# A four-layer float32 transformer pass: the second attention's keys, ones, residuals, token sums and score banks rearranged

## What is computed

```python
x = x + L0_attention(layernorm(x))          # one head of width 256
x = x + L0_experts(layernorm(x))            # 12 experts, top 3; each sequence's output is scaled by 0.2
                                            # where sigmoid(relu(mean_tokens(out) @ Wp1 + bp1) @ Wp2 + bp2) > 0.7
x = x + L1_attention(layernorm(x), kv_k, kv_v)   # 16 heads of width 16 over 4096 given keys
x = x + L1_experts(layernorm(x))            # 8 experts, top 2, and a shared one

# L1_attention
Q = (query @ Wq.T) in heads;  scores = Q K^T / 4;  out = softmax(scores) V;  return out @ Wo.T
```

## Time and profile before

| | |
|---|---|
| median of 3 runs | 2233.84 us (2232.94 to 2234.01) |
| profiled execution | 2250.17 us, its span 2248.4 us |
| busy in the span | PE 2017.5 us, DVE 1573.8, ACT 1361.0, POOL 260.1 |
| mean granted TensorE clock | 0.930 of 2.4 GHz |
| costliest groups | DVE maxima 1241.2 us (1024 of 1224 ns), ACT exponentials 1108.4 (2048 of 595 ns), PE values 650.8, scores 523.6, maxima products 438.5 |

### The profile page before, as it was taken

The page is one execution under the profiler, slowest core; times in us unless marked ns, Lnnn a source line. Parts: engine busy times, 40 slices in busy tenths (PEclk is TensorE's granted clock), DMA queues, the critical chain, the costliest instruction groups (busy, mean ns, idle before and its releaser), DMA issues. The chain is left out here.

```text
span 2248.4 us, 40077 instructions
## 1 busy us (share of the span) xinstructions
PE 2017.5 (90%) x15956; PEld 1006.2 (45%) x15956; DVE 1573.8 (70%) x1951; ACT 1361.0 (61%) x2700; POOL 260.1 (12%) x274
## 2 busy tenths in 40 slices
PE   6793999992478999999999999999999999999984
PEld 3552889991222333333333333333333333446663
DVE  2337212215587999998999999999999999315344
ACT  1220444440114888887888888888888888673221
POOL 0000434431020000000000000000000000002462
PEclk9795999995665999999999999999999999999997
DMA  4201677765815000006100006000002000001124
GB/s 139 84 5 66 211 227 255 254 193 138 107 45 69 6 9 13 13 1 69 13 1 14 13 1 69 13 2 13 13 18 64 2 2 1 17 16 34 59 83 154
DMA packets 150034, 140.93 MB, mean 63 GB/s; under 512 B 75506, under 2 KB 122590, under 8 KB 149086
## 3 DMA queue, kind: packets, MB, share of 16 engines
q1 hardware_dynamic: 140446, 112.72, 21.3%
q0 software_dynamic: 9408, 25.70, 3.5%
HBM read 106.40 MB, written 31.72 MB: 61 GB/s over the span
## 5 line engine op out<-in xcount | busy, mean ns | idle before, releaser
L1003 DVE TENSOR_REDUCE maxp<-banks 128x2 f32<-128x1024 f32 x1024 | 1241.2, 1224 | 73.8 <-PE banks L997 72.8
L1435 ACT ACTIVATE pring<-banks 128x512 f32<-128x512 f32 x2048 | 1108.4, 595 | 231.1 <-PE banks L1316 117.6
L1330 PE MATMUL banks<-pring,vcur 128*17 128x256 f32 x8192 | 650.8, 390 | 7.9 <-ACT osb L1429 3.6
L1316 PE MATMUL banks<-qst,kst 50*128 50x512 f32 x2048 | 523.6, 502 | 6.9 <-PEq L1074 5.4
L997 PE MATMUL banks<-kst,qst 48*128 48x512 f32 x2048 | 438.5, 426 | 29.6 <-DVE maxp L1003 26.4
L1316 PEld LDWEIGHTS banks<-qst,kst 50*128 50x128 f32 x2048 | 199.3, 185 | 448.7 <-ACT pring L1435 416.4
L1330 PEld LDWEIGHTS banks<-pring,vcur 128*17 128x17 f32 x8192 | 137.1, 96 | 369.2 <-issue 202.6
L997 PEld LDWEIGHTS banks<-kst,qst 48*128 48x128 f32 x2048 | 202.1, 194 | 76.7 <-DVE maxp L1003 68.8
L766 ACT ACTIVATE hT<-banks,b 128x128 f32<-128x128 f32 x295 | 108.1, 367 | 187.8 <-PE banks L703 172.2
L904 DVE TENSOR_SCALAR yo<-banks,wblock 128x256 f32<-128x256 f32 x59 | 28.5, 484 | 223.8 <-PE banks L712 223.8
L1301 POOL TENSOR_TENSOR acc<-xn,orec 128x256 f32<-128x256 f32 x15 | 9.3, 620 | 1254.9 <-DVE orec L1480 1254.9
(11 more groups left out here) (304 smaller groups left out, 1306.0 us busy)
## 6 DMA issues: line engine op xcount, KB each, us to landing
w1r<-in_L_ffn_w SPq DMA_DIRECT2D x59, 640.0 KB
kst<-key_parts SPq DMA_DIRECT2D x24, 512.0 KB, 17.6
key_parts<-ksp SPq DMA_DIRECT2D x32, 256.0 KB
w2all<-in_L_ffn_w SPq DMA_DIRECT2D x12, 640.0 KB, 7.7
w2all<-expert_rows SPq DMA_DIRECT2D x12, 512.0 KB, 8.7
qst<-query_parts SPq DMA_DIRECT2D x96, 64.0 KB, 2.3
normed_rows<-xn SPq DMA_DIRECT2D x8, 512.0 KB, 2.9
kf<-in_kT SPq DMA_DIRECT2D x16, 256.0 KB
```

Of the source, the lines that this page charges most:

```text
L1003: return nc.vector.tensor_reduce(maxp[:, B % 2, :, hp, qt, kb], ps[:, base:base + 2, :], X, ALU.max)
L1316: nc.tensor.matmul(ps[:, n % 3, :], kst[g % 2][rows, j // 2, kt * P:(kt + 1) * P], qst[i][rows, j // 2, :], start=True, stop=True).then_in ...
L1330: mm = nc.tensor.matmul(ps[32 * j:32 * j + VC, 7, cols], vcur[g % 2][:, kt, j, :], pring[:, (G % 2) * HG + j, cols], start=(kt == 0 and ha ...
L1435: nc.scalar.activation(pring[:, n % (2 * HG), :], ps[:, n % 3, :], ACT.Exp, scale=float(DH) ** -0.5).then_inc(exp_done, 1)
```

## The change

- The token sums: VectorE's four reductions into `xn` go; TensorE sums `acc` over tokens in the experts' block, one group of eight products with a column of ones for each sequence, once its adds are done.
- The keys: no fill by Pool; two small transfers per key tile bring the ones rows from the `ones` tile. SP starts the keys of group 0 as the first thing in attention 2's block, a quarter of their columns first (`keys_in0`), the rest behind (`keys_in1`, waited for at unit 4). The queries' stores follow; the values are loaded behind sequence 1's store.
- The residuals: sequence 0's stay on VectorE, those of sequences 1 to 3 go to Pool as one multiplication and one addition over 1024 columns each.
- The query split reads PSUM directly; sequence 0's is VectorE's alone.
- STATS stays; APPLY and PIECE of sequences 2 and 3 move back by two units.
- The row maxima of batch 0 are turned and split in the main block, which begins with that turn and with five of the 64 units for batch 1; the first scores wait for the maxima's rows.
- In the last batch the scores have five banks (0 to 4) and the units one (5), so that each unit waits for the previous one.
- 36 more semaphores are cleared at the end of attention 2.

The diff, cut to its core (indentation reduced):

```diff
@@ -746,6 +747,12 @@
                             mm = nc.tensor.matmul(ps[:, SB, i * D:(i + 1) * D], cwT[:, t * P:(t + 1) * P], b2[:], start=True, stop=True)
                         mm.then_inc(bias_mm, 1)
                     output(b, experts[b % LOADED])
+                for c in range(NB):
+                    pe.wait_ge(sums_done, c + 1)
+                    for m in range(KD):
+                        for i in range(TB):
+                            nc.tensor.matmul(ps[:, XB, m * NB + c:m * NB + c + 1], acc[:, TB * c + i, m * P:(m + 1) * P],
+                                             ones[:, 0:1], start=(i == 0), stop=(i == TB - 1))
             @block.scalar
             def _(act):
...
                     for k in range(TOP0):
-                        ch(tt(acc[:, tiles, :], acc[:, tiles, :], sums[c][:, k], ALU.add))
+                        w = tt(acc[:, tiles, :], acc[:, tiles, :], sums[c][:, k], ALU.add)
                         if k < TOP0 - 1:
+                            ch(w)
                             ch.wait()
-                    ch.wait()
-                    nc.vector.tensor_reduce(xn[:, c, :], acc[:, tiles, :].rearrange("p t d -> p d t"), X, ALU.add)
-        clear(step, *route0_sems, *fill_sems, *block_sems, *xg_in, *w1_in, *y_out, *sums_in)
+                    w.then_inc(sums_done, 1)
+        clear(step, sums_done, *route0_sems, *fill_sems, *block_sems, *xg_in, *w1_in, *y_out, *sums_in)
 wgate = sb("wgate", [P, KD, E1 + 1])
...
+    def load_ones(sp, i, done):
+        for r in range(2):
+            row = r * HALF + SIDE * DH
+            sp.dma_start(f32(kst[i][row:row + QP]).rearrange("o h c -> o (h c)").rearrange("o (n c) -> o n c", c=P),
+                         ones[0:QP, :].unsqueeze(1).to_broadcast([QP, NP * KEYS // P, P])).then_inc(done, 16)
+
+    def load_keys(sp, i, g, done, cols=slice(0, KEYS)):
         for r in range(2):
             for s in range(SIDE):
                 src = kparts[K_PART[s]].rearrange("(q a r) c -> a r q c", a=2, r=DH)[r, :, g * NP:(g + 1) * NP, :]
-                sp.dma_start(f32(kst[i][r * HALF + s * DH:r * HALF + (s + 1) * DH]), src).then_inc(done, 16)
+                sp.dma_start(f32(kst[i][r * HALF + s * DH:r * HALF + (s + 1) * DH, :, cols]), src[:, :, cols]).then_inc(done, 16)
...
+        def take_queries(act, b):
             for m in range(KD):
...
+                if m == 0:
+                    act.wait_ge(q_stored, 16 * KD * b)
+                nc.scalar.copy(qsp[:, 0, m], ps[:, 2 + m, :]).then_inc(q_split, 1)
+                if b >= 2:
+                    act.wait_ge(q_left, KD * (b - 1) + m + 1)
                 nc.scalar.copy(qf[:, m, :], ps[:, 2 + m, :]).then_inc(q_taken, 1)
-                if split:
-                    act.wait_ge(q_stored, 16 * KD * b)
-                    for s in range(QP):
-                        if s:
-                            act.wait_ge(q_left, (QP - 1) * (KD * b + m) + s)
-                        else:
-                            act.wait_ge(q_taken, KD * b + m + 1)
-                        nc.scalar.copy(qsp[:, s, m], qf[:, m]).then_inc(q_split, 1)
...
+        def leave(eng, ops, b, m):
+
+            eng.wait_ge(q_split, KD * b + m + 1)
+            eng.wait_ge(q_taken, KD * (b - 1) + m + 1)
+            ops.tensor_tensor(qsp[:, 1, m], qf[:, m], f32(qsp[:, 0, m]), ALU.subtract).then_inc(q_left, 1)
...
+        FEW = KEYS // 4
...
         STATS = {12: 2, 30: 3}
-        APPLY = {14: 2, 32: 3}
-        PIECE = {u0 + (i if i < TB else 5 + 2 * (i - TB)): (n, i) for u0, n in ((0, 1), (16, 2), (34, 3)) for i in range(TB + KD)}
-
...
+        APPLY = {16: 2, 34: 3}
+        PIECE = {u0 + (i if i < TB else 5 + 2 * (i - TB)): (n, i) for u0, n in ((0, 1), (18, 2), (36, 3)) for i in range(TB + KD)}
...
-                sp.wait_ge(ones_set, 1)
-                load_keys(sp, 0, 0, keys_in0)
-                store_queries(sp, 0)
-                for h in range(HG):
-                    load_values(sp, 0, h)
-                for b in range(1, NB):
+                load_ones(sp, 0, keys_in0)
+                load_keys(sp, 0, 0, keys_in0, slice(0, FEW))
+                load_keys(sp, 0, 0, keys_in1, slice(FEW, KEYS))
+                for b in range(NB):
                     store_queries(sp, b)
+                    if b == 1:
+                        for h in range(HG):
+                            load_values(sp, 0, h)
...
-                sp.wait_ge(rows_ready, 1)
-                load_maxima(sp, 0)
-                sp.wait_ge(rows_in, 16 * 2 * QP)
...
-                nc.gpsimd.memset(f32(kst[0][:]), 1.0).then_inc(ones_set, 1)
                 norm_pool(pool, 0, main)
-                for b in range(1, NB):
-                    norm_pool(pool, b, main)
-                    for m in range(KD):
-                        for s in range(QP - 1):
-                            leave(pool, nc.gpsimd, b, m, s)
                 for i in range(2):
                     nc.gpsimd.memset(vcur[i][:, :, :, DH], 1.0)
-                nc.gpsimd.memset(f32(kst[1][:]), 1.0)
+                pool.wait_ge(fac_done, 1)
+                for b in range(1, NB):
+                    tiles = slice(TB * b, TB * (b + 1))
+                    nc.gpsimd.tensor_scalar(acc[:, tiles, :], acc[:, tiles, :], fac[:, b:b + 1], None, ALU.mult).then_inc(scaled, 1)
+                    pool.wait_ge(scaled, b)
+                    nc.gpsimd.tensor_tensor(x[:, tiles, :], x[:, tiles, :], acc[:, tiles, :], ALU.add).then_inc(x_done, 1)
+                    if b == 1:
+                        norm_pool(pool, 1, main)
...
+                for b in range(1, NB):
+                    if b > 1:
+                        norm_pool(pool, b, main)
+                    for m in range(KD):
+                        leave(pool, nc.gpsimd, b, m)
...
-                for m in range(KD):
-                    for b in range(NB):
-                        mm = nc.tensor.matmul(ps[:, 0, m * NB + b:m * NB + b + 1], xn[:, b, m * P:(m + 1) * P],
-                                              ones[:, 0:1], start=True, stop=True)
-                mm.then_inc(phi_mm, 1)
...
-                pe.wait_ge(keys_in0, 16 * 2 * SIDE)
+                pe.wait_ge(keys_in0, 16 * (2 * SIDE + 2))
...
+                                if b == 1:
+                                    pe.wait_ge(q_left, KD)
+                                else:
+                                    pe.wait_ge(q_taken, KD * (b - 1))
...
+                    if u == 4:
+                        pe.wait_ge(keys_in1, 16 * 2 * SIDE)
                     max_unit(u, 0, kst[0], 4 + 2 * (u % 2)).then_inc(max_mm, 1)
-                pe.wait_ge(max_done, 1)
-                nc.tensor.transpose(ps[0:HG * TB, 0, 0:P], mneg[:], ident[:]).then_inc(max_turned, 1)
...
                 def stats_of(b):
-                    residual(dve, b)
...
                     norm_stats(dve, b, lambda t: x[:, TB * b + t, :], main)
...
+                for t in range(TB):
+                    ch(nc.vector.scalar_tensor_tensor(out=x[:, t, :], in0=acc[:, t, :], scalar=fac[:, 0:1],
+                                                      in1=x[:, t, :], op0=ALU.mult, op1=ALU.add))
+                ch.wait()
...
+                for m in range(KD):
+                    dve.wait_ge(q_mm, m + 1)
+                    nc.vector.tensor_copy(qsp[:, 0, m], ps[:, 2 + m, :]).then_inc(q_split, 1)
+                    dve.wait_ge(q_split, m + 1)
+                    nc.vector.tensor_tensor(qsp[:, 1, m], ps[:, 2 + m, :], f32(qsp[:, 0, m]), ALU.subtract).then_inc(q_left, 1)
+                dve.wait_ge(x_done, 1)
...
-                for m in range(KD):
-                    dve.wait_ge(q_taken, m + 1)
-                    for s in range(QP):
-                        nc.vector.tensor_copy(qsp[:, s, m], qf[:, m]).then_inc(q_split, 1)
-                        if s < QP - 1:
-                            leave(dve, nc.vector, 0, m, s)
-                            dve.wait_ge(q_left, (QP - 1) * m + s + 1)
...
+                        dve.wait_ge(x_done, STATS[u])
                         stats_of(STATS[u])
...
                 max_total(0).then_inc(max_done, 1)
-                dve.wait_ge(max_turned, 1)
-                src = ps[0:HG * TB, 0, 0:P]
-                for s in range(QP):
-                    w = nc.vector.tensor_copy(mrow[:, s, :], src)
-                    if s < QP - 1:
-                        ch(w)
-                        ch.wait()
-                        ch(nc.vector.tensor_tensor(mres[:], src, f32(mrow[:, s, :]), ALU.subtract))
-                        ch.wait()
-                        src = mres[:]
-                w.then_inc(rows_ready, 1)
...
+            done = 0 if B else EARLY
+            for u in range(done, NU):
+                plan[begin + (u - done) * (end - begin) // (NU - done)].append(("max", B + 1, u))
...
+    EARLY = 5
     plan = schedule()
+    first = [("turn_max", 0, 0)] + [("max", 1, u) for u in range(EARLY)]
```

(39 more changed lines are left out.)

75 lines of the change are left out of this document (34 added, 41 removed).

## The result

The changed kernel takes 2216.9 us (median of four runs, 2213.75 to 2222.04), the kernel before 2233.39 beside it: a ratio of 0.9929, 95% interval 0.9909 to 0.9948, so 16.5 us faster (12 to 20). Forecast were 2219.3 and 14.5. Its profiled execution took 2222.04 us, span 2220.3; before's 2250.17 and 2248.4.

What follows compares the result with a forecast made beforehand. TensorE and VectorE, nearly always busy, bound attention 2's steady batches; the change touches only the two ends. 7.7 + 3.3 + 1.3 + 2.9 - 0.7 = 14.5 us off 2233.84 gives 2219.3, range 2208 to 2228 with two rivals.

Steps and rivals of the forecast that it cites:

- (a): Token sums ahead of attention 2: four VectorE reductions of 1.88 us go (7.5 us), so the next block begins at 545.85.
- (b): Key load at attention 2's start: ones by transfer instead of Pool's fill; keys start at 547.2, 7.7 us before 554.89.
- (c): First key issue to TensorE's start: loading keys in columns earns nothing; the stretch stays 35.1 us.
- Rival 1: Start of attention 2: the first query store overtakes the keys, TensorE starts at 573; 10 us more gained, 2209; chance 0.12.
- (d): Batch 0's reduction loop: residuals on Pool take 8 of 16 instructions off VectorE, 3.3 us gained; Pool's holds hidden by slack.
- (e): From the total into batch 0: first scores 7.5 us behind it against 5.9, loses 1.6; five early units gain 2.9.
- (f): Last batch, five score banks: 0.20 us at 22 units gains 4.4, one stall costs 1.5; net 2.9 us gained.
- (g): End of attention 2: clearing 36 more semaphores costs 0 to 1.2 us, taken as 0.7.
- rival 2: Start of batch 0: full clock comes at once, saving the 12.3 us that 29 us at 1.2 GHz cost; 2207; chance 0.08.

## Why the prediction came out

The size was right, and partly for another reason than it gave. By its own steps:

- (a) and (b), 7.7 us: measured 5.8. The keys start 7.1 us sooner, counted from the sum loads. Most of the missing part is in the sentence "I take 0, since the stream is bound by its bytes": the ones' own transfer was put between 0 and 3.8 us, and with the cut into pieces it costs 1.4. Undone one at a time, the removal of the reductions is worth 1.2 us and that of the fill, with the pieces, 5.0.
- (c), nothing for the columns: right. The 35.1 us from first key issue to first unit came back as 35.0 without the ones and the pieces. Rival 1, the store that overtakes the keys, did not come; a store placed ahead of half of them showed what it would have been worth: 11.0 us in the profile, 9.0 in the medians, forecast 10.
- (d), 3.3 us: right, 94.8 to 91.5. Pool's hold on VectorE is there (0.8 and 1.6 us on two normalisations) and hidden by the wait for the queries, as it said. Pool's multiplications took 2.9 us, more than the 2.5 that it had as the upper bound; that cost nothing.
- (e), a loss of 1.6 and a gain of 2.9: measured 1.0 against before (7.1 less 6.1) and 2.8. The way was the forecast's, one reduction ahead of the subtraction; it was 0.6 shorter up to the transfers (2.9 us from the total's end to their issue, 3.5 forecast), and the transfers took their 3.9.
- (f), 2.9: 0.20 a unit and one stall of 1.54 are both there; 2.4 for the whole batch at like clock.
- (g), 0.7: 0.8 (from the last osb to the last stage 3.10 before, 3.86 in the run with half of the keys first, both at full clock).
- Not in the forecast: the clock at the start of batch 0. 29.0 and 29.2 us low in the two executions of before; 14.0, 24.3, 14.0, 20.2, 13.7 and 13.5 in the six with five early units and all keys ahead of the store, and 7.3 to 18.4 with the half keys. 12.5 us less on average, at 0.37, are 4.6 us. This is rival 2 by half, to which the prediction gave 0.08. Its price for a low microsecond, 0.43, was a little high: it took a half step at either clock, and batch 0 as a whole has 0.37.

Together: 5.8 + 3.3 - 1.0 + 2.8 + 2.4 - 0.8 = 12.5 us of the edits' own, and 4.6 of the clock in batch 0: 17.1, against 16.5 measured. But this sum leaves out the clock of the last batch, which was low for 36 and 20 us in two profiles of the changed kernel and for 3 and 24 in those of before. The clocks of all runs give the better account. The changed kernel is low for 18.5 us less; some 11 of these lie between the sum loads and the total (143 us low there before, 132 after, two profiles each), where the time was cut while TensorE waited for others; the other 7.5 are 3 us at 0.39. By this estimate 12.5 and about 3 make 15.5, and the means of the runs differ by 15.4 (plus or minus 4).

The forecast's 14.5 was 2.0 too high on the edits and had nothing of the clock: that the two errors nearly cancel is luck.

Why the low stretch became shorter is not settled. It is no one part: without early units, with the residuals, the sums or the fill put back, or with three banks it stays at 12 to 20 us. Solid 48-row work ahead of it did not shorten it, and full-array work moved it. Two executions of the changed kernel differ by 10 us in it, the other kernels among themselves by 8, so that one profile each can't rank them. The runs without early units are low for 14 us more as a whole, so the early units may well have a part in it. A shift of the whole timeline in time might look like this too, but no run here tested it.

## What to carry to other kernels

A small store on a queue costs what was issued ahead of it: put it, with its dependent load, between the pieces of the big one, and cut the big one where its first use needs it. That was worth more here (9 us) than starting the big one 7 us sooner (5.8). An edit ahead of a queued stream is worth only what it moves the stream's issue. And compare profiles stretch by stretch before explaining a span: 19 of 28 us lay in a stage that nobody had changed. A profile is one execution: look where its time lies among the runs of its kernel, and compare the granted clocks of all of them, before a rival is called dead.

## What the hardware showed that was not expected

- TensorE busy 18.7 of 20 us with 48-row float32r products stayed at 0.52; within 5.3 us of full-array float32 products the clock rose; in the score and value products that followed it fell again after 5 us, and 10 us later it rose by itself.
- VectorE's gp, 128x4, took 5.37 us beside Pool's fill, 1.79 in before and 0.23 when Pool rested: in both it ended when the fill did.
- The last batch's low time differs from one execution to the next of the same kernel (3 and 24 us in before, 36 and 20 in the changed one), and the batch's length with it, by 7 us in both pairs. Over the 29 runs of before the mean granted clock accounts for nearly all of the spread: a standard deviation of 6.7 us, 1.3 when 0.39 us for each low one is taken off.
